# Silu made of Tanh and two VectorE operations, with a new order of ScalarE's work, in a fused attention and expert kernel

## The reference

```python
xf = _rms(x, n2_w).reshape(-1, C)
logits = jnp.nan_to_num(xf @ gate_w.T)
probs = jax.nn.softmax(logits, axis=-1)        # top 2 of 4 are kept
o0 = _gelu(xf @ e0_up.T) @ e0_down.T
o1 = jax.nn.silu(xf @ e1_w1.T) * (xf @ e1_w2.T) @ e1_down.T
o2 = _gelu(_gelu(_gelu(xf @ e2_l1.T) @ e2_l2.T) @ e2_l3.T) @ e2_l4.T
o3 = _gelu(_gelu(xf @ e3_down.T) @ e3_up.T) @ e3_out.T
moe = wts[:, 0:1]*o0 + wts[:, 1:2]*o1 + wts[:, 2:3]*o2 + wts[:, 3:4]*o3
```

## Time and profile before

| | us |
|---|---|
| median of 3 runs | 1033.89 |
| lowest, highest | 1033.15, 1034.67 |
| the profiled execution | 1039.72 |
| its span | 1038.0 |

### The profile page before, as it was taken

How to read it: one execution, slowest core, us unless ns; L and a number is a source line. 1 busy time by engine, 2 the same in 40 slices (tenths; PEclk the granted TensorE clock), 3 DMA queues, 4 the chain that set the end, 5 groups by cost and what they waited for, 6 DMA issues and landing times.

```text
span 1038.0 us, 16461 instructions
## 1 busy us (share of the span) xinstructions
PE 888.4 (86%) x6192; PEld 530.8 (51%) x6192; DVE 493.7 (48%) x1123; ACT 545.9 (53%) x1088; POOL 368.8 (36%) x595
## 2 busy tenths in 40 slices
PE   2666878989889989999999999998998999889867
PEld 1545644554456555555556554655463545344434
DVE  1244365545743773476437653566355623441021
ACT  1425316535765576656566655666564474236325
POOL 5314304334523553254324533363233313120312
PEclk9567657768899999998899969998998596558559
DMA  5000000000000000000000000000000000000000
GB/s 157 1 11 1 1 11 1 2 1 12 1 2 1 22 2 1 2 21 2 1 2 22 1 1 2 12 2 2 1 11 2 1 1 11 1 1 0 11 1 10
DMA packets 13725, 9.05 MB, mean 9 GB/s; under 512 B 2128, under 2 KB 13136, under 8 KB 13648
## 3 DMA queue, kind: packets, MB, share of 16 engines
q1 hardware_dynamic: 13648, 8.00, 2.7%
HBM read 5.64 MB, written 2.10 MB: 7 GB/s over the span
## 4 chain that ended last, share of the span: by engine, by line
PE 68%; DVE 14%; ACT 10%; issue 5%; POOL 2%; DMA 1%; SPq 0%; POOLq 0%; ACTq 0%; DVEq 0%
PE side L473 13%; PE outs L410 10%; DVE mneg L880 8%; PE side L359 7%; PE scores L390 6%; PE maxima L372 6%; PE maxima L375 5%; PE side L510 4%; PE outs L449 4%; PE side L461 4%; PE side L430 4%; ACT p L657 4%; PE side L456 3%; DVE p L890 1%; ACT L670 1%
## 5 line engine op out<-in xcount | busy, mean ns | idle before, releaser
L880 DVE TENSOR_REDUCE mneg<-maxima 128x2 f32<-128x256 f32 (+3 forms) x256 | 211.3, 825 | 229.2 <-PE maxima L375 226.0
L657 ACT ACTIVATE p<-scores 128x1024 f32<-128x1024 f32 (+3 forms) x256 | 180.0, 703 | 147.5 <-PE scores L390 146.8
L1104 POOL TENSOR_SCALAR_AFFINE_SELECT p<-p 128x256 f32<-128x256 f32 x256 | 108.3, 424 | 356.6 <-ACT p L657 355.8
L390 PE MATMUL scores<-qs,ks 25*128 25x256 f32 (+3 forms) x512 | 119.7, 464 | 33.4 <-ACT p L657 32.2
L372 PE MATMUL maxima<-ks,qs 24*128 24x384 f32 (+3 forms) x512 | 105.9, 410 | 29.8 <-DVE mneg L880 28.8
L410 PE MATMUL outs<-p,v2x 128*32 128x512 f32 (+3 forms) x1024 | 113.0, 571 | 1.0 <-POOL p L1104 1.0
L390 PEld LDWEIGHTS scores<-qs,ks 25*128 25x128 f32 x512 | 53.9, 207 | 107.2 <-ACT p L657 67.4
L1112 POOL TENSOR_SCALAR_AFFINE_SELECT p<-p 128x512 f32<-128x512 f32 x64 | 40.8, 638 | 157.5 <-ACT p L666 157.5
L890 DVE TENSOR_TENSOR p<-side,sb_t_tri 128x512 f32<-128x512 f32 x64 | 44.2, 690 | 109.9 <-PE side L430 109.8
L372 PEld LDWEIGHTS maxima<-ks,qs 24*128 24x128 f32 x512 | 55.8, 215 | 56.4 <-DVE mneg L880 53.6
L375 PE MATMUL maxima<-negb,idb 128*128 128x128 bf16 x512 | 80.1, 243 | 0.0
(11 more groups left out here) (155 smaller groups left out, 1465.8 us busy)
## 6 DMA issues: line engine op xcount, KB each, us to landing
x_in<-x_dram SPq DMA_DIRECT2D x8, 256.0 KB, 2.9
qs<-mT SPq DMA_DIRECT2D x128, 2.0 KB
out_dram<-yout SPq DMA_DIRECT2D x8, 256.0 KB, 2.3
sb_t_cos<-t_cos_dram SPq DMA_DIRECT2D x1, 512.0 KB, 5.2
sb_t_sin<-t_sin_dram SPq DMA_DIRECT2D x1, 512.0 KB, 5.1
sb_w_l<-w_l_dram SPq DMA_DIRECT2D x2, 256.0 KB
sb_w_qkv<-w_qkv_dram SPq DMA_DIRECT2D x2, 192.0 KB, 4.6
sb_w_u<-w_u_dram SPq DMA_DIRECT2D x3, 128.0 KB
```

The source lines that it names most:

```text
L390: last = nc.tensor.matmul(eb[:, i, 0:n], ks[rows, b % 2, g, 128 * kt:128 * kt + 128], qs[rows, b % 2, g, 128 * kt:T], start=True, stop=True)
L657: A_(p2[kt][:, 2 * hp:2 * hp + 2, :], eb[:, :, 0:n], ACT.Exp, scale=float(D) ** -0.5).then_inc(exp_done, 1)
L880: V.tensor_reduce(mneg[:, g, 2 * hp:2 * hp + 2, qt], mb[:, :, 0:128 * (qt + 1)], AX.X, ALU.max, negate=True)\
L1104: Q.affine_select(out=diag, in_=diag, compare_op=ALU.is_ge, fill=0.0, base=0, pattern=[[0, 2], [1, 128]], channel_multiplier=-1).then_inc( ...
```

## The change

- Expert 1: ScalarE makes tanh(G/2) instead of silu(G). VectorE makes (tanh + 1) * G from it, then half of that times U; both are fused operations of three operands. The buffer of G is now free only after VectorE's first operation (`g_read`), not after ScalarE's.
- The routing Exp moves from place 3 to place 0, behind the copies S200 and S201, and right behind it a Gelu of one number per partition is added. Behind the last Gelu of place 6 an Exp of one number per partition is added.
- The four accumulating Squares become one Square of all 512 columns (step 25, into nat2) and a reduction on VectorE at step 26; VectorE's and GpSimd's work that follows moves from step 27 to 26.
- `high` moves from steps 18 and 19 to 19 and 20, `low` from 18 and 20 to 20 and 22. The transposes S1 with their copies stand at 21 (two), 22, 24 (two), 25, 26 and 28. The transpose N21 moves from step 21 to 20.

In the diff, the first `experts` is ScalarE's and the second VectorE's.

```diff
-    NF + 20: [(2, "S110"), (2, "S111")],
-    NF + 21: [(2, "S112"), (2, "S113"), (-1, "N21")],
-    NF + 22: [(2, "S100"), (-1, "AO")],
+    NF + 20: [(-1, "N21")],
+    NF + 21: [(2, "S110"), (2, "S111")],
+    NF + 22: [(2, "S112"), (-1, "AO")],
     NF + 23: [(-1, "WO2")],
-    NF + 24: [(2, "S101")],
-    NF + 25: [(0, "MT2")],
+    NF + 24: [(2, "S113"), (2, "S100")],
+    NF + 25: [(0, "MT2"), (2, "S101")],
...
             def experts(b, place, half=None):
                 if place in (0, 1):
-                    hidden(f"G{place}", b, sil[:, place, :], ACT.Silu)
+                    src = side(f"G{place}", b)
+                    A_(sil[:, place, :], src[:, :], ACT.Tanh, scale=0.5).then_inc(h_ready, 1)
...
                         hidden(f"U0{m}", b, h0[:, m, :], ACT.Gelu)
+                    A_(switched[:, 2:3], ident[:, 0:1], ACT.Exp)
...
-                if s == 18:
+                if s == 19:
                     high(1).then_inc(high1_ready, 1)
-                if s == 19:
+                if s == 20:
                     high(0).then_inc(high1_ready, 1)
...
-                    for t in (0, 1) if s == 25 else (2, 3):
-                        i = A_(weighted[:, t, 0:2, 0:C // 2], z[:, b % 3, t, :].rearrange("p (e c) -> p e c", e=2), ACT.Square, accum_out=gsum[:, t:t + 1])
-                    i.then_inc(ysq_ready, 1)
+                    A_(nat2[:], z[:, b % 3], ACT.Square).then_inc(ysq_ready, 1)
...
-                    if place == 3 and on(it - 2):
-                        tail(it - 2, G * GK)
...
                         before(it, G * GK + place)
+                    if place == 0 and on(it - 2):
+                        tail(it - 2, G * GK)
+                        A_(switched[:, 0:1], ident[:, 0:1], ACT.Gelu)
...
             def experts(b, place):
                 if place in (0, 1):
+                    gate = side(f"G{place}", b)
+                    dve.wait_ge(h_ready, count(h_ready, b, 1 + place))
+                    V.scalar_tensor_tensor(sil[:, place, :], sil[:, place, :], 1.0, gate[:], ALU.add, ALU.mult).then_inc(g_read, 1)
                     src = side(f"U{place}", b)
-                    dve.wait_ge(h_ready, count(h_ready, b, 1 + place))
-                    V.tensor_tensor(h1[:, place, :], src[:], sil[:, place, :], ALU.mult).then_inc(h1_ready, 1)
+                    dve.wait_ge(g_read, count(g_read, b, 1 + place))
+                    V.scalar_tensor_tensor(h1[:, place, :], sil[:, place, :], 0.5, src[:], ALU.mult, ALU.mult).then_inc(h1_ready, 1)
...
-                if s == 27:
-                    dve.wait_ge(ysq_ready, count(ysq_ready, b, 2))
+                if s == 26:
+                    dve.wait_ge(ysq_ready, count(ysq_ready, b, 1))
+                    step(V.tensor_reduce(gsum[:], nat2[:], AX.X, ALU.add))
```

More of the change, by code:

```diff
@@ L77 @@
 SPLIT2_AT = {29: (1, 0, 1), 30: (1, 1, 2), 31: (1, 2, 4), 32: (0, 0, 2), 33: (0, 2, 4)}
-SPLIT1_AT = {20: (1, 0, 2), 21: (1, 2, 4), 22: (0, 0, 1), 24: (0, 1, 2), 26: (0, 2, 3), 28: (0, 3, 4)}
+SPLIT1_AT = {21: ((1, 0, 2),), 22: ((1, 2, 3),), 24: ((1, 3, 4), (0, 0, 1)), 25: ((0, 1, 2),), 26: ((0, 2, 3),), 28: ((0, 3, 4),)}
 FILLED = []
@@ L218, in build @@
         gsum = sb("gsum", [128, NT])
+        switched = sb("switched", [128, 3])
         wts = sb("wts", [128, NT, E])
@@ L285, in build @@
         y_ready = counted("y_ready")
-        ysq_ready = counted("ysq_ready", 2)
+        ysq_ready = counted("ysq_ready")
         base_ready = counted("base_ready")
@@ L295, in build @@
         h1_ready = counted("h1_ready", 2)
+        g_read = counted("g_read", 2)
         down_read = counted("down_read", NT)
@@ L315, in build @@
         SIDE_READ = {"N20": (n2_read, 1), "N21": (n2_read, 2), "AO": (aoT_ready, 1), "WO2": (y_ready, 1), "XF": (xfT_ready, 1),
-                     "GATE": (logits_read, 1), "G0": (h_ready, 1), "G1": (h_ready, 2), "U0": (h1_ready, 1), "U1": (h1_ready, 2),
+                     "GATE": (logits_read, 1), "G0": (g_read, 1), "G1": (g_read, 2), "U0": (h1_ready, 1), "U1": (h1_ready, 2),
                      "L10": (h_ready, 3), "L11": (h_ready, 4), "D3": (h_ready, 5), "L20": (h_ready, 6), "L21": (h_ready, 7),
@@ L562, in lead @@
                 if s in SPLIT1_AT:
[L563 to L566, removed]
+                    for n, g0, g1 in SPLIT1_AT[s]:
+                        pe.wait_ge(high1_ready, count(high1_ready, b, 2 - n))
+                        pe.wait_ge(low1_ready, count(low1_ready, b, 4 - 2 * n))
+                        split(b, 1, n, g0, g1)
             def tail(b, s):
-                if s in (13, 21):
-                    x = (s - 13) // 8
+                if s in (13, 20):
+                    x = (s - 13) // 7
                     dst = side(f"N2{x}", b)
@@ L767, in lead @@
                     A_(qT[:, :], src[:, :], ACT.Copy).then_inc(qT_ready, 1)
-                if s == 18:
+                if s == 19:
                     high(1).then_inc(high1_ready, 1)
-                if s == 19:
+                if s == 20:
                     high(0).then_inc(high1_ready, 1)
                 if s in SPLIT1_AT:
[L773 to L776, removed]
+                    for n, g0, g1 in SPLIT1_AT[s]:
+                        for g in range(g0, g1):
+                            src = side(f"S1{n}{g}", b)
+                            A_((qs1, ks1)[n][:, g, :], src[:, :], ACT.Copy).then_inc((copied1_a, copied1_b)[g % 2], 1)
             def tail(b, s):
@@ L781, in tail @@
                     A_(aoT[:, :], src[:, :], ACT.Copy).then_inc(aoT_ready, 1)
-                if s in (25, 26):
+                if s == 25:
                     act.wait_ge(y_ready, count(y_ready, b, 1))
-                    if b:
-                        act.wait_ge(out_ready, count(out_ready, b, 0))
-                    for t in (0, 1) if s == 25 else (2, 3):
-                        i = A_(weighted[:, t, 0:2, 0:C // 2], z[:, b % 3, t, :].rearrange("p (e c) -> p e c", e=2), ACT.Square, accum_out=gsum[:, t:t + 1])
-                    i.then_inc(ysq_ready, 1)
+                    A_(nat2[:], z[:, b % 3], ACT.Square).then_inc(ysq_ready, 1)
                 if s == 30:
@@ L1139, in before @@
                     if s == G * GK + 2 and b >= 3:
-                        pool.wait_ge(ysq_ready, count(ysq_ready, b - 3, 2))
+                        pool.wait_ge(ysq_ready, count(ysq_ready, b - 3, 1))
                         pool.wait_ge(xf_ready, count(xf_ready, b - 3, 1))
@@ L1190, in lead @@
                                     sq.rearrange("p t (s c) -> p t s c", s=2), ALU.add).then_inc(qk1_ready, 1)
-                if s in (18, 20):
-                    n = (20 - s) // 2
+                if s in (20, 22):
+                    n = (22 - s) // 2
                     pool.wait_ge(high1_ready, count(high1_ready, b, 2 - n))
```

## The result

The changed kernel takes 1021.62 us (median of 4 runs, 1019.11 to 1022.96); the kernel before, beside it, 1034.28 (1033.15 to 1034.87). The ratio is 0.9876, interval 0.9855 to 0.9897: 12.7 us faster. I had forecast 4.9 us: the sign was right, the size was not. Where a kernel's executions scatter widely with the clock (e2, e6 and e10), the comparison leaves out those over 1.5% above the fastest, and I give the median and range of all of them instead.

A forecast was written before the change was run, and what follows sets the result against it. The prediction took TensorE, busy for 86% of the span, to set the end. Its terms, -1.6 (expert), +0.6 (late rounds), -2.5 (attention) and -1.4 (clock), summed to -4.9 us, from a median of 1033.9 to 1029, range 1014 to 1042.

The forecast's parts named there:

- Expert part: Places 0 to 3 and step 0: +1.0 +0.54 -1.33 -0.53, so -0.3 us a round, -1.6 in five.
- +1.0 at place 0: TensorE starts SC02 1.0 us later, waiting for Tanh (0.3) and VectorE's fused operation (0.7).
- +0.54: Place 1: L10 starts 0.54 us later still, since reading U1 now stands two VectorE operations behind Tanh.
- -1.33: Places 2 and 3: TensorE's gap of 1.53 us ahead of L21 shrinks to about 0.2.
- the load of 1.28 that leaves step 0: Step 0: the Exp's table load moves behind place 6; TensorE's 0.53 us gap goes, the rest was hidden.
- Late rounds: Expert parts at 832 and 930 us: the load stays on the path, added instructions count; +0.6 us for both.
- Attention part: Steps 16 to 29: step 20's gap goes; -0.5 us a round, bounds -1.85 to +0.4, five rounds -2.5.
- clock term: Round at 466 us: the slow stretch of 2.7 us behind step 20's gap, counted half, -1.4 us.
- The clock holds: Rival, end of the attention part: no clock fall there, 3 us in each of five rounds, 1014 us; chance 0.20.
- The clock falls at place 0: Rival: the gap doubled to 2.0 us costs 2.7 to 3.0 us a fall; 1041 with four; chance 0.18.
- VectorE did not set the pace: Rival, steps 24 to 29: VectorE sets the pace, +1.0 us a round in seven rounds, about 1036; chance 0.15.
- Tanh needed no load: Rival, place 0: Tanh needs its own table load, +1.3 and about +1.0 us a round, 1039; chance 0.05.

The follow-up runs named there:

- e2: The kernel before with only the new order of high, low, the S1 transposes and N21: 1026.4 us (1007.9 to 1028.9).
- e6: The whole change with three unread products in TensorE's wait at place 0: 1026.2 us (1004.8 to 1039.8).
- e10: The whole change with unread products ahead of the scores of steps 27 and 28 and two at place 0: 1010.8 us (992.8 to 1012.7).
- e13: The kernel before with unread products at place 0, steps 15, 20, 27, 28 and in the late rounds: 992.7 us, ratio 0.956.
- e14: The whole change with unread products at place 0 (two), steps 15, 27, 28 and in the late rounds: 995.2 us, ratio 0.960.
- e9: The kernel before with only unread products ahead of the scores of steps 27 and 28: 1017.5 us, ratio 0.981.
- e5: The whole change once more, unaltered, against the kernel before: 1018.9 us, ratio 0.981.
- e1: The kernel before with only the expert part of the change (Tanh, fused operations, routing Exp, one-number instructions): 1041.7 us, ratio 1.004.
- e7: The whole change with Silu kept, plus unread products ahead of the scores of steps 27 and 28: 1006.0 us, ratio 0.970.
- e11: As e7, plus one unread product at place 0 and one at step 15: 997.3 us, ratio 0.961.

## Why the forecast had the sign and missed the size

- **Expert part: right.** The wait ahead of SC02 is 1.96 us (2.0 forecast), VectorE's operation 0.69, the wait ahead of SC12 0.71 at full clock (0.6), the one ahead of L21 0.25 (under 0.4). The forecast's +1.0 at place 0 is e's +1.00; its +0.54, -1.33 and the load of 1.28 that leaves step 0, together -2.07, are f's -2.08; the 0.75 of that load that it took as hidden comes back in a's +0.83. In all -0.25 a round against -0.3.
- **Late rounds: too small.** For the two late expert parts (832 and 930 us) +0.6 was forecast; by e13 and e14 the late rounds are some 2.5 us longer at full clock. Most of it is f of the expert part that stands at 930 in before, 1.26 longer with TensorE's wait of 0.63 us for VectorE, which the sum did not have; +0.8 in a and +0.7 in d of the round before come next. The last expert part, forecast at 0, is right: from its first product to the end of the program 32.75 us before and 32.59 after.
- **Attention part: right in kind.** c and d together give -0.8 a round against -0.5, inside the bounds; step 20's wait went and those of steps 27 and 28 are 0.76 and 0.57.
- **The clock: the step that failed.** The sum's clock term was -1.4, half of one fall in one round ("The same gap in other rounds brought no fall, so I count half"). It priced only the fall behind the gap of step 20; those behind steps 25 to 29 stood in a rival, and those ahead of and behind the steady rounds nowhere. The measured pair has -12.7, of which length accounts for some -2.5, so some -10 are clock. e9 shows the size: the clock behind steps 27 and 28 alone, held in the kernel before, is worth as much as the whole change (0.981). e13 against e14 shows the rest: with the products in both, -12.7 has become +2.5. In the profiled pair the falls cost less in d and e (-4.1 us) and c (-1.5), more in f (+0.5), and 7.3 less in the last attention part. Which falls an execution has is not fixed by the program (one program, after and e5, has 3 and 5 of them in f and reaches the first steady round at 216.3 and 211.5 us), so the share of each could not be settled; that the greater part is clock is shown.
- **Luck.** That the sign came right and 1021.6 lies inside the stated range owes little to the sum: its terms other than the clock gave -3.5, of which some -2.5 are there, and the clock might have gone the other way, as it did in e1, where the path is shorter too and the time 4 us longer.
- **The rivals.** "The clock holds" did not come about by the change itself (e stays at 0.60 to 0.91); its price of 3 us a round was near what the products bring (107.2 to 104.2 in e9). "The clock falls at place 0" did come true, in 8 of the 10 rounds of after and e5 and in all of e1, and filling the wait ended it (e6, e10, e14), but a fall there costs 1.3 us in most rounds and at most 2.3, not 2.7 to 3.0. The Trainium skill, "TensorE: Matmul & The Clock Gate", section "A second HAM failure mode: psum-queue depth-cycling", describes such a swing of the clock behind short idle times; e6, e7 and e11 agree in that the falls went where these were filled (f at 1.00 in e6, e in e7, c and f in e11). VectorE did not set the pace: in the steady rounds no wait of TensorE for its maxima in steps 27 and 28 is listed. Its sum was off, too: 1029 + 7 + 3 is 1039, not 1036. Tanh needed no load: 17 loads, none at Tanh. The Trainium skill, "ScalarE: Activation LUTs", section "Table sets: the hidden batching unit", lists tanh with exp and with sigmoid and not with gelu; here the set that Gelu had loaded served it.

## What to carry to other kernels

Keep two accounts: compare lengths only between stretches that both ran at full clock, and count falls of the clock apart, over several rounds and several executions, the first and last parts included. Where TensorE waits in thin work (here 0.5 to 2 us), a product that nobody reads, put into that wait, costs little and is a test as well as a remedy: in the kernel before it gave more (1038.6 to 992.7) than all changes of order and operations. It is no guarantee: e14's c fell to 0.65 in a round with these products. A change that was weighed with the clock free should be weighed again with it held.

## What was not expected of the hardware

- The same wait lets the clock fall in one round and not in the next. In e7 TensorE waits 0.62 us ahead of the maxima of step 15 in both rounds whose c stands above, and one ran at 0.84 and the other at 1.00; in e13 and e14 the waits around step 15 of the last round are the same (0.58 and 0.40 us), and only e14's clock fell. What else decides is open.
- Executions of one kernel scatter along with the mean granted clock: the kernel before from 1030.3 us at 0.844 to 1043.8 at 0.825, e2 from 1007.9 at 0.856 to 1028.9 at 0.832. A difference of 1% between single executions of two kernels of this sort is within what the clock does.
- A product of 128x512 in these types is two instructions in the trace and takes 0.91 us (2.74 for three).
